# Final projection in groups of eight token tiles instead of four, and a weight queue eight deep instead of six

## The reference

```python
def attn(x):                                  # I = 2048, H = 1024
    p = x @ in_proj_w.T
    h, gate = p[..., :I], silu(p[..., I:])
    h = (causal_group_conv(h, conv_w, K=4, groups=8) + conv_b) * gate
    m = silu(layernorm(h) @ fc_w.T + fc_b) @ cproj_w.T + cproj_b
    return (m + h) @ out_w.T                  # the final projection
def ffn(x):                                   # 4096 hidden
    h = silu(x @ w1.T * s1) * (x @ w2.T * s2)
    h = gelu(h @ h1.T * t1)
    h = gelu(h @ h2.T * t2)
    return h @ w3.T * s3
xn = layernorm(x)
out = x + attn(xn) + ffn(xn)
```

## Time and profile before

| | |
|---|---|
| median of 3 runs | 3915.47 us |
| lowest and highest | 3890.65 and 4434.41 us |
| profiled execution, its time | 3915.47 us |
| its span, slowest core (core 2) | 3913.8 us |
| spans of the eight cores | 3874.7 to 3913.8 us |
| TensorE busy | 3338.5 us, 85% of the span |
| VectorE, ScalarE, GpSimd busy | 548.5, 888.5, 416.2 us |

### The profile page before, as it was taken

The page is one execution under the profiler, slowest core; times in us unless marked ns, Lnnn a source line. Parts: engine busy times, 40 slices in busy tenths (PEclk is TensorE's granted clock), DMA queues, the critical chain, the costliest instruction groups (busy, mean ns, idle before and its releaser), DMA issues.

```text
span 3913.8 us, 38156 instructions; the slowest of 8 cores (3874.7 to 3913.8 us)
## 1 busy us (share of the span) xinstructions
PE 3338.5 (85%) x14744; PEld 1440.2 (37%) x14744; DVE 548.5 (14%) x996; ACT 888.5 (23%) x1007; POOL 416.2 (11%) x791
## 2 busy tenths in 40 slices
PE   3778999999999988899999999998999756656554
PEld 1333344444444433334444444443444212222111
DVE  3221000000000131110000000003232344221111
ACT  2222111111111103321111111110207672241000
POOL 0000000000000120000000000012000001111333
PEclk9778899999999999999999999999999879888877
DMA  3233444444444463344444444445222124445777
GB/s 90 54 59 49 64 76 76 76 76 76 76 76 76 71 108 65 64 69 76 76 78 77 77 77 78 78 66 101 45 37 36 25 38 65 71 66 83 134 153 153
DMA packets 121363, 292.83 MB, mean 75 GB/s; under 512 B 14305, under 2 KB 47202, under 8 KB 121186
## 3 DMA queue, kind: packets, MB, share of 16 engines
q0 software_dynamic: 109232, 264.59, 40.9%
q1 hardware_dynamic: 11954, 25.80, 1.9%
HBM read 521.32 MB, written 16.78 MB: 137 GB/s over the span
## 4 chain that ended last, share of the span: by engine, by line
PE 78%; DMA 9%; issue 4%; ACT 4%; DVE 3%; DVEq 1%; POOL 0%; ACTq 0%; POOLq 0%; SPq 0%
PE ps_mm L489 45%; PE ps_mm L420 13%; PE ps_mm L657 3%; PE ps_mm L701 3%; PE ps_mm L734 3%; DMA ab<-cprojT 3%; PE ps_mm L543 3%; PE ps_tok L543 3%; DMA ab<-outwR 2%; ACT L863 2%; PE ps_mm L815 2%; PE ps_mm L787 2%; DMA af<-x 1%; DVE ab L449 1%; DMA ab<-fcT 1%
## 5 line engine op out<-in xcount | busy, mean ns | idle before, releaser
L489 PE MATMUL ps_mm<-ab 128*128 128x512 bf16 x8192 | 1784.1, 381 | 8.2 <-DVE ab L449 4.2
L489 PEld LDWEIGHTS ps_mm<-ab 128*128 128x128 bf16 x8192 | 803.1, 98 | 989.3 <-issue 59.7
L420 PE MATMUL ps_mm<-ab 128*128 128x512 bf16 x2048 | 500.6, 407 | 62.9 <-DVE ab L449 61.8
L503 ACT ACT_TABLE_LOAD x128 | 164.2, 1283 | 817.4 <-PE ps_mm L489 817.4
L420 PEld LDWEIGHTS ps_mm<-ab 128*128 128x128 bf16 x2048 | 207.7, 103 | 352.1 <-issue 211.4
L528 DVE TENSOR_TENSOR ab<-ab 128x512 bf16<-128x512 bf16 x128 | 54.4, 425 | 1958.5 <-DMA ab<-w3R 1887.5
L503 ACT ACTIVATE ab<-ps_mm,params_s 128x512 bf16<-128x512 f32 x256 | 175.9, 687 | 638.7 <-PE ps_mm L489 637.2
L815 PE MATMUL ps_mm<-ab 128*128 128x512 bf16 x512 | 132.8, 409 | 94.6 <-DMA ab<-cprojT 83.4
L787 PE MATMUL ps_mm<-ab 128*128 128x512 bf16 x512 | 141.7, 445 | 72.8 <-ACT ab L797 44.8
L435 ACT ACT_TABLE_LOAD x64 | 82.1, 1283 | 529.1 <-PE ps_mm L420 529.1
L449 DVE SCALAR_TENSOR_TENSOR ab<-ps_mm,params_s,ab 128x512 bf16<-128x512 f32 x128 | 96.1, 751 | 464.0 <-PE ps_mm L420 458.1
(11 more groups left out here) (73 smaller groups left out, 1664.0 us busy)
## 6 DMA issues: line engine op xcount, KB each, us to landing
ab<-h1T POOLq DMA_DIRECT2D x128, 512.0 KB, 5.8
ab<-h2T POOLq DMA_DIRECT2D x128, 512.0 KB, 5.7
ab<-w12T POOLq DMA_DIRECT2D x64, 512.0 KB, 5.1
ab<-w3R POOLq DMA_DIRECT2D x128, 128.0 KB, 3.0
ab<-fcT POOLq DMA_DIRECT2D x32, 512.0 KB, 5.7
ab<-cprojT POOLq DMA_DIRECT2D x64, 256.0 KB, 4.0
ab<-outwR POOLq DMA_DIRECT2D x128, 128.0 KB, 3.7
af<-x SPq DMA_DIRECT2D x17, 512.0 KB, 3.5
```

What stands on the lines that cost most here:

```text
L420: ins = tensor.matmul(ps_mm[bank][:, 0:NT], pan3[:, k, :], xn(k, c0 + t2 * NT, NT), start=(k == 0), stop=(k == HC - 1))
L489: ins = tensor.matmul(ps_mm[bank][:, 0:NT], pan3[:, kk, :], src_t(k, t2 * NT, NT), start=(k == 0), stop=(k == FC - 1))
L503: ins = scalar.activation(dst_t(m, t2 * NT, NT), ps_mm[bank][:, 0:NT], AF.Gelu, bias=0.0, scale=params[:, psc + m:psc + m + 1])
```

## The change

The final projection takes groups of eight token tiles instead of four: two groups instead of four, each on all eight banks, so `bb` disappears. The weight pieces are then read twice instead of four times: 64 loads instead of 128, each followed by eight matmuls instead of four. The number of matmuls (512) and of evictions (32) stays. The list of POOL, the order of evictions and the order of stores are regrouped the same way. NWQ goes from 6 to 8. An added wait for store ii-2 on VectorE repeats one that stands a few lines above it; `_wait_ge` drops it, and no instruction comes of it.

```diff
-    NWQ = 6
+    NWQ = 8
...
-        for grp in range(n_g4):
+        for grp in range(n_grp):
             for half in range(2):
                 for kc in range(IC):
                     sl = kc % 4
                     wadd(f"ow_{grp}_{half}_{kc}", ring(r_owp, sl, 512),
...
-                for tc in range(grp * 4, min((grp + 1) * 4, n_tc)):
+                for tc in range(grp * 8, min((grp + 1) * 8, n_tc)):
                     ii = _fin.index((grp, half, tc))
                     wadd(f"acc_{tc}_{half}",
...
-    for grp in range(n_g4):
-        tcs = list(range(grp * 4, min((grp + 1) * 4, n_tc)))
+    for grp in range(n_grp):
+        tcs = list(range(grp * 8, min((grp + 1) * 8, n_tc)))
         need_nt = (tcs[-1] * 128 + 127) // NT
-        bb = (grp % 2) * 4
         for half in range(2):
...
                         if kc == 0:
-                            bank_wait(tensor, bb + j)
+                            bank_wait(tensor, j)
                         ins = tensor.matmul(
-                            ps8[bb + j], rc_t(kc, tc * 128, 128), pan,
+                            ps8[j], rc_t(kc, tc * 128, 128), pan,
                             start=(kc == 0), stop=(kc == IC - 1))
...
+                    if ii >= 2:
+                        pg2, ph2, pt2 = fin_order[ii - 2]
+                        saq_wait(vector, f"ost_{pt2}_{ph2}")
                     vector.drain()
-                    vector.scalar_tensor_tensor(osts, ps8[bb + j], 1.0, accs,
+                    vector.scalar_tensor_tensor(osts, ps8[j], 1.0, accs,
                                                 ALU.mult, ALU.add)
```

More of the change, by code:

```diff
@@ L253, in build_program @@
                      r_cpp + (m % 2) * 1024, 1024)
-    n_g4 = (n_tc + 3) // 4
     if trunc is None:
         _fin = []
-        for grp in range(n_g4):
+        for grp in range(n_grp):
             for half in range(2):
-                for tc in range(grp * 4, min((grp + 1) * 4, n_tc)):
+                for tc in range(grp * 8, min((grp + 1) * 8, n_tc)):
                     _fin.append((grp, half, tc))
-        for grp in range(n_g4):
+        for grp in range(n_grp):
             for half in range(2):
@@ L594, in _ @@
                     tc2, half2 = int(tc2), int(half2)
-                    ii = fin_idx[(tc2 // 4, half2, tc2)]
+                    ii = fin_idx[(tc2 // 8, half2, tc2)]
                     if ii == 0 and pre == "acc":
@@ L983, in build_program, with _ @@
              kind="store", data_mark=f"ost_{tc}_{half}")
-    for grp in range(n_g4):
-        tcs = list(range(grp * 4, min((grp + 1) * 4, n_tc)))
+    for grp in range(n_grp):
+        tcs = list(range(grp * 8, min((grp + 1) * 8, n_tc)))
         need_nt = (tcs[-1] * 128 + 127) // NT
-        bb = (grp % 2) * 4
         for half in range(2):
             @block.tensor
-            def _(tensor, grp=grp, half=half, tcs=tcs, need_nt=need_nt, bb=bb):
+            def _(tensor, grp=grp, half=half, tcs=tcs, need_nt=need_nt):
                 if half == 0:
@@ L1010, in _ @@
                 @block.vector
-                def _(vector, grp=grp, half=half, j=j, tc=tc, bb=bb):
+                def _(vector, grp=grp, half=half, j=j, tc=tc):
                     ii = fin_idx[(grp, half, tc)]
@@ L1032, in _ @@
                     mark(f"ibk_{tc}_{half}", s_v, v)
-                    bank_done(bb + j, f"ibk_{tc}_{half}")
+                    bank_done(j, f"ibk_{tc}_{half}")
     _emit_dma_queues()
```

## The result

| | before | after |
|---|---|---|
| median, lowest of all runs | 3895.95 us, 3884.01 us (11 runs) | 3835.91 us, 3825.37 us (9 runs) |
| profiled execution, span | 3915.47 us, 3913.8 us | 3835.23 us, 3833.7 us |
| final projection, mean of the eight cores | 289.3 us | 232.0 us |

The ratio of the two kernels, run side by side, is 0.9842 with a 95% interval from 0.9817 to 0.9867: some 60 us faster. (Now and then all cores of a die run at a lower clock; the ratios leave such runs out.) The forecast was 48 us and a ratio of 0.988, so the time lies in the stated range and within 2%, but 1.6% is clear of no change: this kernel can be measured to a quarter of a per cent, and the 2% of the prediction was too coarse.

The account below looks back on a forecast made before the run. It took the final projection as a chain of waits, mostly for weight pieces, with no engine full. Stretches 121.5 + gaps 80.1 + tail 29.0 = 230.6 us against 278.8; 48.2 less than 3915.47 gives 3867.3 us, range 3825 to 3905.

Parts of the forecast that it names:

- stretches: Final projection, TensorE's runs of matmuls between long gaps: eight of 22.5 us become four of 28.5 or 31.0 us.
- gaps: TensorE's long idle times between stretches: seven of 12.0 us become three of 26.7 us, each two eviction cycles longer.
- tail: From the last matmul to the span's end: four eviction pairs instead of two, 14.3 us become 29.0.
- The start at the low clock: Matmuls behind a gap begin at 1.2 GHz: 2.5 us added to each of the three stretches after the first.
- three pieces ahead cover 5.2 us: In the new stretches, three weight pieces of 1.73 us work each cover a landing 3.0 us after issue.
- The cycle: Time for one pair of evictions, from its first to the next pair's first: 7.9 us, counted eight times.
- the 1.1 us that should have come off: Delay from last matmul to first eviction, expected to vanish from each gap and the tail as loads land earlier.
- quick cycles: Rival: eviction cycles fall to 5.6 us as DMA engines are less loaded; 66.6 us saved, 3849 us; chance 0.12.
- The banks: Each new stretch needs the banks just filled: put at nothing, or 1 us at each of three gaps.
- NWQ: Weight queue depth from 6 to 8: put at zero, at most 1 us a gap either way.
- Nothing gained: Rival: evictions eat the whole gain, with a cycle of 13.9 us; 3915 us; chance 0.05.
- clock low: Rival: TensorE stays at 1.2 GHz after the longer gaps; 72 us more, 3939 us; chance 0.03.

Follow-up runs that it names:

- experiments 6 and 7: Changed kernel, every weight piece loaded twice: ratio 0.9839; then kernel before with sixteen weight slots instead of four: 0.9866, and changed kernel with two: 1.0033.
- experiment 3: Changed kernel with the next stretch's first four weight pieces issued behind the second pair's loads instead of the fourth's: ratio to the kernel before 0.9793.
- experiments 1 and 2: NWQ alone: kernel before with 8 instead of 6, ratio 1.0001; changed kernel with 6 instead of 8, ratio to the kernel before 0.9779.
- experiment 1: Kernel before with NWQ 8 instead of 6 and nothing else: ratio 1.0001, final projection 288.8 us against 289.3.

## Why the prediction was right, and where it was not

| term, us | forecast, core 2 | before, mean of 8 | after, mean of 8 |
|---|---|---|---|
| stretches | 180.3 to 121.5 | 187.7 | 119.1 |
| gaps | 84.2 to 80.1 | 87.0 | 83.5 |
| tail | 14.3 to 29.0 | 14.6 | 29.3 |
| stage | 278.8 to 230.6 | 289.3 | 232.0 |

**The stretches of matmuls.** Right, with its model: w3's 28.5 us for 128 matmuls against 28.3 for the first stretch, and 29.7 to 30.2 where 31.0 stood. The start at the low clock was put a little high. The prediction read the 1.4 us a piece of before but not why it is so; experiments 6 and 7 show that it is the round trip of a slot and not the delivery, and its own "three pieces ahead cover 5.2 us" was that argument half made.

**The gaps and the tail.** Right in kind and within 3.4 us in sum: three gaps of 27.8 us in the mean of the cores where 26.7 stood, a tail of 29.3 for 29.0. The cycle, the largest unknown, is 8.2, 7.5 and 6.9 us for the first, second and third in a row on core 2. The pieces are issued 5.0 us behind the fifth eviction (3643.05 to 3648.03) as they were 4.6 us behind the first in the earlier trace rows, so the two cycles that were added are the first and the second: 15.7 us on core 2, and 15.8 was forecast. The terms of a gap in the mean of all eight cores:

| us | before | after |
|---|---|---|
| last matmul to first eviction | 1.1 | 0.9 |
| added cycles | none | 15.2 |
| first (now fifth) eviction to issue of the piece | 5.0 | 5.7 |
| issue to TensorE's start | 6.3 | 6.0 |
| gap | 12.4 | 27.8 |

The term that was mis-sized is the 1.1 us that should have come off: 0.2 did. In the first and third gap the evictions begin 0.3 to 0.5 us behind the last matmul on core 2, in the second 3.7 us behind it (1.1 to 3.7 on the eight cores); there POOL stood still for 2.6 us before it issued the loads for the first pair, at 3681.99, with no releaser named, and why is open. The forecast is a little closer than its terms: its cycle of 7.9 us is core 2's, where the eight cores have 7.4 us before and 7.5 after. The Trainium skill, DMA: Bandwidth & Descriptors, section on the anatomy of one DMA on the GpSimd path, gave an estimate of 2.6 us for a load of 256 KB; after the change `acc` and `xr` land in 4.6 and 5.2 us in the median, so the row was the better guide, and the quick cycles did not come.

**The banks** were put at nothing, and the gaps show nothing of them. But experiment 3 shows that this was a narrow thing: take the late piece away and the banks hold TensorE just as long. **NWQ** at zero: borne out by experiments 1 and 2, in both kernels, within their intervals. **The clock**: behind the 24 gaps of 25.6 to 30.7 us on the eight cores TensorE left 1.2 GHz 2.9 to 5.9 us after its restart, behind the 56 gaps of before, of 10.7 to 15.1 us, after 2.5 to 5.9 us; so the warning of TensorE: Matmul & The Clock Gate, section Seeing it yourself, in the Trainium skill, of a clock stuck low, is not met in any run here. **The added wait** has no part of its own in the trace.

**The steps that failed.** The mechanism held, and two steps of the reckoning did not. The first is the reading of what can be seen at all: "A measurement of this kernel can tell about 2% from no change, that is 78 us" had no row behind it, and with it the prediction forecast, at 0.93, a result that can't be told from no change. The result does lie within 2%, but the interval of the runs side by side is a quarter of a per cent to each side, some 10 us, and the kernel is 1.6% faster. The 48 us of the forecast would have been clear as well.

The second is the side of before. "The stage runs from the first matmul at 3634.99 to the end of the span at 3913.8, which is 278.8 us" was read on one core, and that core happened to have the shortest stage of the eight (278.8 to 300.1 us). In the mean it is 289.3, 10.5 us more: 7.4 in the stretches, 2.8 in the gaps, 0.3 in the tail. From 289.3 to 232.0 is 57.3 us, not 48.2. Without cores 0 and 1 and their low clock the stage before is 286.4 us: from 286.4 to 232.0, 54.4 us.

With it goes the sum's base: in the profiled execution, 3915.47 us, cores 2 and 3 carried the 43 to 45 us that they had lost by 1331 us, as experiment 1 told. Of the seven runs of the kernel before that count for the ratio the six others lie between 3884.0 and 3896.0 us, 3891.2 in the mean. From there less 57.3 the forecast would have been 3833.9 us; the changed kernel's mean over such runs is 3833.1. So the 3867.3 us were 33.4 too high, 24.3 from the base and 9.1 from the gain, and the stage accounts for nearly all of the difference between the kernels (58.1 us from 3891.2 to 3833.1), whether it is taken as 57.3 or 54.4 us. That these last sums meet within 1 us is partly luck, since the stages are those of one execution each.

**The rivals.** Quick cycles: no, although its 3849 us lies near the result; the cycles are 7.5 us in the mean, and the time came from elsewhere. Nothing gained and clock low: no.

Left open: why core 2 has a short stage in before. A late start, with the neighbours finished earlier, is an obvious guess, but with NWQ = 8 core 2 started in among the others (3598.1, the cores lie between 3585 and 3611) and was again the shortest (281.3 of 281.3 to 294.2 us); in the changed kernel it was the longest (236.1).

## What to carry to other kernels

A ring of n slots that is refilled on use delivers at most n pieces in one round trip, even where the DMA engines could do more (shown here with two and four slots): before counting bytes, divide the trip from use to landed refill by the slots and compare it with the work that a piece feeds. To use a piece for more work, or to add slots, both cure it, but a group that fills all banks side by side makes all evictions fall due at once; to finish one bank after another, with the weights resident, removed gaps and refills alike. And before a time is taken from one profiled core, the same stage is to be read on all eight, and the slowest core's early stages to be compared with its neighbours'.

## What the runs showed of the hardware that was not expected

- A landing is no constant: a piece of 128 KB lands in 3.0 us with two slots, in 3.2 in the changed kernel, and in 5.4 and 5.5 us with sixteen slots or double loads, while pieces come out more often (one in 2.86, and one in 1.03 or 1.04 us). In these runs more loads under way went with a longer landing and a higher rate.
- Two cores of one die can run one stage of one execution at a granted clock of 0.80 or 0.86 where their neighbours have 0.93: cores 2 and 3 in one execution, 34 us late at the end of that stage and 45 and 43 us later on, and cores 6 and 7 in another, some 17 us late. Later in the first of these executions it was cores 0 and 1 that had 0.81, for 122 and 112 us of the final projection, and cores 2 and 3 did not.
- A gap of 26 to 31 us costs the clock about what one of 11 to 15 does: behind it 10.8 matmuls run at 1.2 GHz in the mean of the eight cores, behind the shorter gaps of before 10.1. On core 2 a stretch took 1.4 to 1.9 us more than the first one (29.7 to 30.2 us against 28.3); of the 24 matmuls behind 11.35 us in the earlier trace rows, which took 3.1 us more than at full speed, 14 ran at 1.2 GHz, and that is 3.0 us.
